# A finer work list for a mixture-of-experts tail: one more level, one chunk fetched earlier, six tiles weighed on another engine

## What is computed

```python
x = x + attention(layernorm(x))       # causal, scores of width 1024, one softmax per token
x = x + moe(layernorm(x))             # 8 experts, top 2, SwiGLU with hidden size 256
# moe: scores = softmax(x @ gate_w.T); the two best experts of each token;
#      y = (silu(x @ w1[e]) * (x @ w3[e])) @ w2[e]; out[token] += y * score
```

## Time and profile before

| | |
|---|---|
| times of three runs | 238.39, 239.30, 239.92 us; median 239.3 us |
| the profiled execution | 239.59 us, of which the span is 237.8 us and 1.8 us lie around it |
| granted TensorE clock | 0.994 of full speed |
| busy share of the span | PE 95%, DVE 79%, POOL 69%, ACT 61% |
| indirect DMAs of POOL | 65 stores and 64 scatters, 1.0 us each |
| DMA traffic | 28.95 MB, 122 GB/s over the span |

### The profile page before, as it was taken

One profiled execution on the slowest core, in us unless ns is written; L12 is line 12 of the kernel. 1 busy time (PEld: TensorE's weight loads), 2 busy tenths in 40 slices (PEclk: granted clock), 3 DMA queues, 4 the chain that ended last, 5 costly groups with the idle time before them and its releaser, 6 DMA issues.

```text
span 237.8 us, 6363 instructions
## 1 busy us (share of the span) xinstructions
PE 225.1 (95%) x1794; PEld 206.4 (87%) x1795; DVE 187.6 (79%) x851; ACT 145.8 (61%) x391; POOL 163.3 (69%) x204
## 2 busy tenths in 40 slices
PE   7989999999999999999999999999999999999960
PEld 6978888898799767877999998889999999999960
DVE  2479898879897789977898799957675656699994
ACT  2267787777877757855699665556575656566300
POOL 6523337788888888868577777777777777777700
PEclk9999999999999999999999999999999999999997
DMA  7999801111111111115124425534333333598368
GB/s 224 305 320 335 234 5 36 36 37 46 34 50 36 48 40 41 46 37 136 37 75 108 108 82 129 127 96 124 94 110 103 101 90 102 165 331 274 102 192 276
DMA packets 31978, 28.95 MB, mean 122 GB/s; under 512 B 4152, under 2 KB 26560, under 8 KB 31952
## 3 DMA queue, kind: packets, MB, share of 16 engines
q1 hardware_dynamic: 25216, 18.60, 28.5%
q0 software_dynamic: 4128, 8.59, 10.8%
q10 hardware_dynamic: 2608, 1.45, 2.0%
HBM read 16.34 MB, written 12.29 MB: 120 GB/s over the span
## 4 chain that ended last, share of the span: by engine, by line
PE 79%; POOL 6%; DMA 5%; DVE 3%; ACT 2%; issue 2%; ACTq 1%; POOLq 1%
PE scores L747 12%; PE turned L747 12%; PE scores L619 12%; PE weighed L680 11%; PE scores L768 6%; PE turned L645 5%; POOL expert_rows L524 4%; PE mixed L768 3%; PE weighed L768 3%; PE mixed L634 3%; PE mixed L633 3%; DMA choice_rows<-ysb,ycol 2%; DMA TL<-choice_rows 2%; DMA TL<-L_attn_w_o 2%; PE scores L764 2%
## 5 line engine op out<-in xcount | busy, mean ns | idle before, releaser
L535 POOL DMA_INDIRECT choice_rows<-ysb,ycol x65 | 65.0, 999 | 19.8 <-issue 14.6
L524 POOL DMA_INDIRECT expert_rows<-rows,slots x64 | 64.4, 1007 | 18.2 <-issue 13.2
L884 ACT ACTIVATE Wt<-W 128x512 f32 x71 | 44.1, 625 | 15.7 <-issue 15.7
L747 PE MATMUL scores<-xT,Wt 128*128 128x128 f32 x288 | 38.2, 276 | 0.8 <-issue 0.8
L619 PE MATMUL scores<-XX,TL 128*128 128x512 f32 (+3 forms) x96 | 38.1, 506 | 0.2 <-ACT TL L857 0.2
L680 PE MATMUL weighed<-TL,PT 128*128 128x136 f32 x272 | 37.0, 281 | 0.8 <-DVE X L1008 0.7
L747 PE MATMUL turned<-xT,Wt 128*128 128x128 f32 x280 | 37.1, 275 | 0.0
L747 PEld LDWEIGHTS scores<-xT,Wt 128*128 128x128 f32 x288 | 35.0, 192 | 1.1 <-issue 1.1
L680 PEld LDWEIGHTS weighed<-TL,PT 128*128 128x128 f32 x272 | 33.7, 190 | 1.7 <-issue 1.6
L747 PEld LDWEIGHTS turned<-xT,Wt 128*128 128x128 f32 x280 | 34.1, 192 | 0.0
L996 DVE TENSOR_REDUCE negmax<-scores 128x1 f32<-128x128 f32 (+7 forms) x32 | 23.5, 734 | 5.0 <-PE scores L619 5.0
(11 more groups left out here) (182 smaller groups left out, 456.1 us busy)
## 6 DMA issues: line engine op xcount, KB each, us to landing
xt<-expert_rows SPq DMA_DIRECT2D x71, 66.0 KB
TL<-choice_rows SPq DMA_DIRECT2D x15, 256.0 KB, 3.9
W<-L_ffn_w SPq DMA_DIRECT2D x2, 1024.0 KB, 9.7
out<-X ACTq DMA_DIRECT2D x9, 128.0 KB
choice_rows<-ysb,ycol POOLq DMA_INDIRECT x65, 2.3
X<-L_attn_in_features SPq DMA_DIRECT2D x2, 512.0 KB, 7.5
expert_rows<-rows,slots POOLq DMA_INDIRECT x64
out<-X SPq DMA_DIRECT2D x5, 128.0 KB
```

What stands on the lines that cost most here:

```text
L524: nc.gpsimd.indirect_dma_start(xs, bass.IndirectOffsetOnAxis(ap=slots[:, u, k:k + 1], axis=0), rows[:, u % ROWS_RING, k, :], None).then_in ...
L535: nc.gpsimd.indirect_dma_start(yb, bass.IndirectOffsetOnAxis(ap=ycol[:, q, 0:1].bitcast(u32), axis=0), ysb[:, q, :], None).then_inc(y_out[ ...
L747: mm(bank[2 + j % RING][:, c * P:(c + 1) * P], Wt[:, j % RING, c * P:(c + 1) * P], xT[:, j % RING, :], start=True, stop=True)
L884: copy(Wt[:, j % RING, :], W[:, ds(w * (SET // WIDE), SET)], ACT.Copy).then_inc(Wt_rdy, 1)
```

## The change

It has three parts.

1. LEVELS gets group 5 (MID) between groups 4 and 6, so SEG is 40. All rows of groups 0 to 5 are then stored after the first SOONER = 55 stores.
2. SP waits for 55 stores and fetches chunk 5 right behind its last load, ahead of the writes of chunks 0 to 2; chunk 6 stays behind the wait for 63.
3. ACT weighs y of the six sown tiles (`weigh_sown`), with a semaphore of its own (`ys_rdy`) for which PE's `sow` and `pair` wait. DVE no longer weighs these tiles, and its additions of chunks 3 to 6 follow one another behind the last tile step.

```diff
--- before.py
+++ after.py
@@ -59,13 +59,14 @@
 ROWS_HALF = K * P * sum(n for _, n in GROUPS[:HALF + 1])
 NT0 = (ROWS_HALF - E * (P - 1)) // P // LANES * LANES
 NEAR = 16
+MID, SOONER = 5, 55
 FAR, LATER = 6, 63
 SOWN = 3
-LEVELS = (HALF, FAR, len(GROUPS) - 1, len(GROUPS) - 1)
+LEVELS = (HALF, MID, FAR, len(GROUPS) - 1, len(GROUPS) - 1)
 SEG = len(LEVELS) * E
 NT1 = LISTED - NT0
 assert (ROWS_HALF + E * (P - 1)) // P - NT0 <= NEAR
-assert (K * P * sum(n for _, n in GROUPS[:FAR + 1]) + E * (P - 1)) // P <= LATER
+assert all((K * P * sum(n for _, n in GROUPS[:l + 1]) + E * (P - 1)) // P <= most for l, most in ((MID, SOONER), (FAR, LATER)))
 assert GROUPS[-1][1] > SOWN
 N_PARTS = 5
 REST_AT = [8, 9, 10, 12, 14, 16, 18]
@@ -235,11 +236,11 @@
         head_mm, step_mm, xT_rdy, sil_rdy, g_rdy = (
             sem("head_mm"), sem("step_mm"), sem("xT_rdy"), sem("sil_rdy"), sem("g_rdy"))
         ycol_rdy = sem("ycol_rdy")
-        Wt_rdy, y_rdy = sem("Wt_rdy"), sem("y_rdy")
+        Wt_rdy, y_rdy, ys_rdy = sem("Wt_rdy"), sem("y_rdy"), sem("ys_rdy")
         y_zero, low_rdy, lowf_rdy, pick_rdy, sown_mm = (
             sem("y_zero"), sem("low_rdy"), sem("lowf_rdy"), sem("pick_rdy"), sem("sown_mm"))
         sum2, last0, last1 = sem("sum2"), sem("last0"), sem("last1")
-        assert NF - N_EARLY == LAG
+        assert MID == HALF + 1 == N_EARLY and FAR == NF - 2
         yf_in = [sem(f"yf_in{j}") for j in range(ZF)]
         sum0, sum1, out_done = sem("sum0"), sem("sum1"), sem("out_done")
         N_DESTS = 2 + (NF - 2) // 2
@@ -440,11 +441,12 @@
                 load(m)
             for m in range(FETCH_AT[0] // LANES, M_TILES):
                 load(m, between=True)
+            stores_in(sp, 0, SOONER)
+            fetch(MID)
             for c in range(N_SOON):
                 write(c)
-            stores_in(sp, 0, LATER)
-            for c in range(N_EARLY, LAST):
-                fetch(c)
+            stores_in(sp, SOONER, LATER)
+            fetch(FAR)
             stores_in(sp, LATER, STORED)
             fetch_last(sp, 0)
             write_last(sp, 0)
@@ -684,7 +686,7 @@
             def sow(t):
 
                 n = t - STORED
-                pe.wait_ge(y_rdy, t + 1)
+                pe.wait_ge(ys_rdy, n + 1)
                 pe.wait_ge(pick_rdy, n + 1)
                 for i in range(SOWN):
                     a, at = sown_at(i)
@@ -756,8 +758,10 @@
                     pe.wait_ge(*((xT_rdy, 2 * t + 2) if t < 2 else (x1_rdy, N_TILES - 1) if b is pO else (place_rdy, NG)))
                 elif static and used < LAG:
                     pe.wait_ge(xT_rdy, used + LEAD + 1)
+                elif not static or used - LAG < STORED:
+                    pe.wait_ge(y_rdy, used - LAG + 1)
                 else:
-                    pe.wait_ge(y_rdy, used - LAG + 1)
+                    pe.wait_ge(ys_rdy, used - LAG - STORED + 1)
                 if not static or t < LAST_TURN:
                     n = (j + LEAD) % LANES
                     pe.wait_ge(xt_in[n], 16 * (m + (j + LEAD) // LANES + 1))
@@ -944,10 +948,24 @@
                     silu(m, j)
             w = weights_of(M_TILES - 1, LANES - AHEAD)
             last = NT - (M_TILES - 1) * LANES
+
+            def weigh_sown(t):
+
+                at = t + LAG
+                act.wait_ge(ycol_rdy, t + 1)
+                act.wait_ge(step_mm, at + 1)
+                copy(ysb[:, t % OUT_LANES, :], bank[pair_bank(at)][:, P:P + D], ACT.Copy,
+                     scale=ycol[:, t % OUT_LANES, 1:2]).then_inc(ys_rdy, 1)
+
             for j in range(last):
+                t = (M_TILES - 1) * LANES + j
                 if j + AHEAD < last:
                     stage(M_TILES - 1, j + AHEAD, w[j])
                 silu(M_TILES - 1, j)
+                if t - LAG >= STORED:
+                    weigh_sown(t - LAG)
+            for t in range(NT - LAG, NT):
+                weigh_sown(t)
 
             stores_in(act, 0, STORED)
             fetch_last(act, 1)
@@ -1221,7 +1239,7 @@
                 if not isinstance(r, int) or t < LAST_TURN:
                     v.tensor_copy(xT[:, (q + LEAD) % RING, :], b[:, 0:P]).then_inc(xT_rdy, 1)
                     keep_places(r + (q + LEAD) // OUT_LANES, (q + LEAD) % OUT_LANES)
-                if not isinstance(r, int) or t >= LAG:
+                if not isinstance(r, int) or LAG <= t < STORED + LAG:
                     n = (q - LAG) % OUT_LANES
                     v.tensor_scalar(ysb[:, n, :], b[:, P:P + D], ycol[:, n, 1:2], None, ALU.mult).then_inc(y_rdy, 1)
 
@@ -1408,12 +1426,7 @@
                 for n in range(2):
                     if STORED <= STORED + 2 * (t - NT + LEAD) + n < NT:
                         picks(STORED + 2 * (t - NT + LEAD) + n)
-            out_pair(*divmod(NT, OUT_LANES))
-            add_choice(N_SOON, 0)
-            out_pair(*divmod(NT + 1, OUT_LANES))
-            add_choice(N_SOON, 1)
-            out_pair(*divmod(NT + 2, OUT_LANES))
-            for c in range(N_SOON + 1, LAST):
+            for c in range(N_SOON, LAST):
                 for k in range(K):
                     add_choice(c, k)
```

## The result

Twenty runs of each kernel, side by side: 241.94 us median after, 239.78 us before; the ratio is 1.0091 with a 95% interval of 1.0063 to 1.0119. The change makes the kernel some 2.2 us slower. That is outside the forecast range (to 241.2 us), though still inside the 1% that the prediction called the same. Its number is that of rival C, which had been given 0.13 and 240.9 to 241.6 us, and a little beyond its price. Of the 2.3 us above the forecast of 239.6 us, 0.5 us lie in its base: it was reckoned from 239.3 us, the median of three runs, and twenty give 239.78.

A forecast was written before the change was run, and what follows sets the result against it. The last store's chain, paced by POOL, was taken as the bound; the list's cost and the tail's gain nearly cancel, +0.3 us (ScalarE's half landing at 233.9 against 233.56) on the 239.3 median: 239.6 us, range 237.8 to 241.2.

The forecast's parts named there:

- rival C: List and tail: stretched POOL falls in step with additions, last store at 226.0 or later; 240.9 to 241.6 us; chance 0.13.
- The bound: Whole kernel: the end hangs on the last store's chain from 224.39, 13.4 us, its start set by POOL's queue.
- after 225.4: Tail: a last store starting later than this time in us was the sign deciding for the slower rival, chance 0.13.
- The list on DVE, +1.75 us, and on POOL, +0.67: Second list, 135 to 153 us: longer operations add 1.75 us on DVE, 0.67 on POOL; PE delayed 1.6.
- "I take 0" for the attention stage: Attention stage: group 5's extra count costs nothing because PE sets the pace; other end 0.2 us.
- The beat, "0.67 to 1.6": Near the end: DVE's additions and picks hold POOL's stores, so the last store starts 0.67 to 1.6 us late.
- So the last store lands in 3.7 us: Tail: with only chunk 6 beside it, landing takes 3.7 us for 4.85, bounds 2.3 and 4.85: -1.15 us.
- ScalarE's late half: Tail: ScalarE issues its half of the last fetch only after its last weighing, at 228.8 or 230.1 instead of 229.26.
- The landing row at 204.9: Earlier profile row, nearest case of one chunk fetched beside a store: 3.7 us, taken as the last store's landing time.
- DVE's cover: Tail: DVE loses six weighings of 0.35 us, so its eight additions begin earlier; this is cover, not path.
- The lock: Port shared by DVE and POOL: whoever issues first keeps it a whole instruction; two SBUF inputs on DVE suffice.

The follow-up runs named there:

- small additions: Kernel after with the six additions of chunks 0 to 2 cut to two columns a token, rest of the sums left out: 240.52 us, ratio 1.0043.
- the old place of the fetch: Kernel after with chunk 5 fetched at its earlier place, group 5's level and ScalarE's weighing kept: 240.65 us, ratio 1.0036; again 240.64 us, 1.0066.
- the last kernels: Kernel before with ScalarE's weighing, second list's operations cut in four, last fetch on SP, chunk 3 added sooner: 237.59 us; with level and early fetch too: 240.43 us.
- the second execution of the same program: Kernel after, unchanged, run once more beside other kernels on one chip: 241.55 us, ratio 1.0084.
- level + weighing: Kernel before with group 5's level and ScalarE's weighing, chunk 5 fetched at its old place: 240.65 us, ratio 1.0036; again 240.64 us, 1.0066.
- after with the list cut: Kernel after with list operations L1128 and L1138 each cut into four pieces of 10 entries: 241.46 us, ratio 1.0071.
- the list cut: Kernel before with list operations L1128 and L1138 each cut into four pieces: 239.87 us, ratio 1.0026.

## Why the prediction was wrong, point by point

- **The bound.** Right: the chain of the last store, paced by POOL, carries the whole difference between these two traces. (In nine of the other fifteen traces DVE's row or ScalarE's half ended last.) It is not the whole of the 2.2 us, though: where the store lands early (small additions, the old place of the fetch) the time falls by 0.9 to 1.4 us only, and some 1 us above before is left. There ScalarE's half ends last, behind a PE that is done 1.9 us later than before. The store did start "after 225.4", the point named for rival C.
- **The list on DVE, +1.75 us, and on POOL, +0.67.** Right: 1.81 and 1.80 us for 1.81 forecast, +0.71 on POOL. PE's last matmul moved from 229.48 to 232.81, 1.92 us beyond the start; 0.40 of that came from the attention stage, so 1.5 for the forecast 1.6.
- **"I take 0" for the attention stage.** Wrong: 0.40 us. The profile's busy PE was taken as cover, but PE waits for L1026 there (0.34 us). From the first maximum to the scatter at 125.01 it is 0.26 to 0.46 us more in every kernel with the level and uncut lists, 0.62 and 0.63 in the two with the level and a cut, and within 0.05 us of before in the two that have neither. The cut of the first list alone costs as much as the level there (0.28 and 0.42 us), which is why the last kernels cut only the second (with four levels that scatter then comes 0.39 us sooner than before). PE's wait for L1026 is the row that I had not looked for.
- **The beat, "0.67 to 1.6".** Right in kind, too small: five stores in step were counted, six came, and the sixth was held for 0.5 us. The beat took 1.21 us for the 0.9 forecast; with the 0.71 of the list and the 0.40 of the attention stage the store started 2.3 us late. The small additions confirm the mechanism.
- **"So the last store lands in 3.7 us".** The step that failed, by its size and by its reason. It took the 4.85 us as the price of four transfers and halved them. Nothing beside gives 2.2, two transfers 3.2 to 3.8, so halving them is worth some 0.3 us and not 1.15; and here an instruction packet held one engine for 1.23 us, and it was 5.13. The landing was forecast at 229.7 and came at 231.8 (233.25 less the 1.41 of the start): 1.4 us are this term, 0.7 the later start. The fetch then took 4.16 for 3.8, and ScalarE's late half, forecast at 0.4, did not come; these two cancel. In the second execution of the same program the landing took 4.4 us and the store started at the same place: 0.7 us are this term there, 0.6 the later start, so its size is not fixed, and the attention stage and the beat weigh as much. Rival C's number came true, but its reason for the landing, that the transfers beside it cost what they did, did not. The landing row at 204.9 had no packet in it, and I didn't look at queue 8.
- **ScalarE's late half.** Without effect in the kernel after, where the store lands last (ScalarE is done 1.4 us ahead of it). It is what ended last wherever weighing and level meet a short landing, as the forecast had it: in level + weighing (both times), small additions, and after with the list cut, 1.3 to 2.3 us behind SP's half.
- **DVE's cover.** Right in the kernel after (2.61 us idle). It is thin, though: 1.3 us off POOL's path in the list cut, and DVE binds.

The lock that the prediction took from the Trainium skill (SBUF — State Buffer, "Who interferes with whom") fits the instructions beside the list's L1146 and L1156 (2.44 and 2.31 us beside 1.81; L1128 and L1138 before) and the additions that begin just ahead of POOL's instruction (1.46). Its "whoever issues first" the page says of VectorE's 2-port modes; the prediction carried it over to two SBUF inputs, and by that an addition that begins 0.19 us behind POOL's should have waited. It takes 0.68 us: there the measurement decides.

## What to carry to other kernels

When a queue runs without a gap, look for what can stretch its pieces, and lay the period of each such operation beside the queue's: here 1.26 us against 1.45 falls into step, and each beat costs 0.2 us. Before moving a transfer away from a landing, split the landing's time by queue in short windows, instruction fetches among them; here one engine, held by one packet, set it. Ask of each variant what ended last, before its time is booked on a cause: in nine of these seventeen traces it was not the chain of the last store. A longer piece of bookkeeping on one partition was dearer than the transfer it let go earlier: count it on every engine that shares its port or waits behind it.

## What the runs showed that was not expected

- A 16 KB instruction packet in the tail occupies one DMA engine for 0.9 to 1.3 us, and a 64 KB indirect store whose last rows stand behind it lands 1 us later.
- A lead of 0.08 us over a 0.68 us addition leaves a POOL instruction at 0.96 us; starting 0.05 us behind makes it 1.46. Held instructions end 0.83 to 0.86 us behind the end of what holds them.
- Two executions of one program can differ by 1 us in the first 10 us alone: the granted TensorE clock was full from 7.04 us on in one and from 9.06 in the other.
